# A hand-written instruction order for the first two batches: scores before maxima products, and norm rows before value transposes

## The reference

```
# layer 0: x is (256, 512) per batch; 8 heads of 32, over 512 positions, masked by cond
q      = x.T @ Wq.T                          # query, key and value are the same
logits = (scale * q q.T masked by key) * query mask
x      = x + (softmax(logits) @ q @ Wo.T).T
# layer 1: rows of x (256 rows of 512); 16 heads of 32
scale, shift = split(cond @ W_emb + b_emb)   # the modulation
xn      = rms_norm(x, g_norm) * (1 + scale) + shift
q, k, v = split(xn @ W_qkv);  q, k = rms_norm per head
x       = x + o + o @ W_out                  # o = softmax(q k.T / sqrt(32)) @ v
```

## Time and profile before

| | |
|---|---|
| median of 3 runs | 1290.88 us (1289.24 to 1292.41) |
| profiled execution | 1290.69 us |
| its span, first to last instruction | 1288.5 us |
| mean granted TensorE clock | 0.981 |
| busy in the span: TensorE, VectorE, ScalarE, GpSimd | 1231.0, 1032.1, 768.5, 771.6 us |
| instructions | 20732 |

### The profile page before, as it was taken

One profiled execution on the slowest core, in us unless ns is written; L12 is line 12 of the kernel. 1 busy time (PEld: TensorE's weight loads), 2 busy tenths in 40 slices (PEclk: granted clock), 3 DMA queues, 4 the chain that ended last, 5 costly groups with the idle time before them and its releaser, 6 DMA issues.

```text
span 1288.5 us, 20732 instructions
## 1 busy us (share of the span) xinstructions
PE 1231.0 (96%) x6769; PEld 577.5 (45%) x6769; DVE 1032.1 (80%) x920; ACT 768.5 (60%) x1394; POOL 771.6 (60%) x387
## 2 busy tenths in 40 slices
PE   3889899999999999999999999999999999999998
PEld 1364444545444454544445454444544444454434
DVE  6666878788887878888787888878888897887664
ACT  1616566766656576665657656565766656566524
POOL 1517566484756748575574857557485755837542
PEclk7969999999999999999999999999999999999999
DMA  5712635435373543536354353635345363533432
GB/s 143 266 34 75 155 92 123 110 88 125 82 171 92 120 111 83 133 82 168 95 117 110 87 132 82 163 97 116 95 102 138 82 161 93 119 91 74 98 73 59
DMA packets 77975, 143.00 MB, mean 111 GB/s; under 512 B 21552, under 2 KB 23088, under 8 KB 77872
## 3 DMA queue, kind: packets, MB, share of 16 engines
q1 hardware_dynamic: 69552, 130.36, 40.5%
q10 hardware_dynamic: 8320, 11.32, 3.3%
HBM read 32.02 MB, written 8.39 MB: 31 GB/s over the span
## 4 chain that ended last, share of the span: by engine, by line
PE 80%; POOL 6%; DVE 4%; issue 3%; ACT 3%; SPq 2%; DMA 1%; ACTq 1%; DVEq 0%; POOLq 0%
PE PX L599 25%; PE PS L501 9%; PE PO L531 8%; PE PX L633 8%; PE PS L518 5%; PE PO L553 5%; POOL RQK L2272 4%; PE PM L464 4%; PE PX L570 2%; PE PM L570 2%; PE PO L556 2%; PE PM L473 2%; SPq L2453 2%; PE PM L542 1%; PE PM L581 1%
## 5 line engine op out<-in xcount | busy, mean ns | idle before, releaser
L1213 ACT ACTIVATE E<-PS,KBIAS 128x512 f32<-128x512 f32 x512 | 340.8, 686 | 195.8 <-PE PS L501 152.6
L599 PE MATMUL PX<-WQKV,XNT 128*128 128x512 f32 x752 | 377.2, 604 | 0.7 <-DVE XNT L1895 0.4
L1822 DVE TENSOR_REDUCE NM<-PM 128x4 f32<-128x2048 f32 x128 | 292.1, 2282 | 72.3 <-PE PM L464 72.3
L2260 POOL TENSOR_TENSOR E<-E 128x1024 f32<-128x1024 f32 x112 | 263.3, 2370 | 88.1 <-PE PO L531 77.8
L501 PE MATMUL PS<-B,A 97*128 97x512 f32 x512 | 287.5, 597 | 4.6 <-ACT E L1213 3.8
L2290 POOL TENSOR_TENSOR KQLO<-E 128x1024 f32<-128x1024 f32 x64 | 151.6, 2368 | 224.4 <-ACT E L1220 222.7
L2272 POOL TENSOR_TENSOR RQK<-RQK,HALF 128x16 f32<-128x16 f32 x64 | 212.8, 3331 | 94.7 <-DVE RQK L1910 94.3
L1220 ACT ACTIVATE E<-PS 128x512 f32<-128x512 f32 x256 | 146.9, 597 | 110.6 <-PE PS L518 110.4
L599 PEld LDWEIGHTS PX<-WQKV,XNT 128*128 128x128 f32 x752 | 134.0, 191 | 99.7 <-issue 89.7
L1829 DVE TENSOR_REDUCE NM<-PM 128x8 f32<-128x2048 f32 x64 | 146.3, 2286 | 37.1 <-PE PM L473 37.1
L501 PEld LDWEIGHTS PS<-B,A 97*128 97x128 f32 x512 | 92.2, 189 | 156.5 <-issue 105.2
(11 more groups left out here) (87 smaller groups left out, 1352.4 us busy)
## 6 DMA issues: line engine op xcount, KB each, us to landing
A<-KQHI SPq DMA_DIRECT2D x126, 128.0 KB, 2.4
B<-KQHI SPq DMA_DIRECT2D x126, 128.0 KB, 2.4
A<-QHI SPq DMA_DIRECT2D x248, 64.0 KB, 2.0
B<-QHI SPq DMA_DIRECT2D x248, 64.0 KB, 2.0
XB<-x SPq DMA_DIRECT2D x16, 512.0 KB, 4.1
X<-x ACTq DMA_DIRECT2D x16, 512.0 KB, 5.0
out<-X1R SPq DMA_DIRECT2D x32, 256.0 KB, 2.9
A<-KQLO SPq DMA_DIRECT2D x63, 128.0 KB, 2.4
```

Source lines behind the costliest of these rows:

```text
L599: last = mm(bank, XNT[:, c, t * P:(t + 1) * P], WQKV[:, c, part * DM:(part + 1) * DM], start=(c == 0), stop=(c == 3))
L1213: fn(E[:, probs(seg, i, g), h, :], PS[n % 2][:, :], ACT.Exp, bias=KBIAS[:, g, b:b + 1], scale=SCALE).then_inc(exp_done, 1)
L1822: v.tensor_reduce(NM0[:, q, :].rearrange("p (h k) -> p h k", k=KB0)[:, :, kb], PM[:, :, :], axis=AX.X, op=ALU.max, negate=True).then_inc(m ...
L2260: g_.tensor_tensor(running(seg, i)[:, heads_, :], running(seg, i)[:, heads_, :], E[:, probs(seg, i, g), heads_, :], ALU.add).then_inc(done, 1)
```

## The change

It edits the order of iterations 0 and 1 on three engines, and the list of the banks' uses to match.

At the start of a batch (batch 0 here), on TensorE: scores 0 and 1 of segment A go in front of the second maxima product of quad 1. The first half of the next batch's query projection, which stood between score 0 and score 1, goes behind the third maxima product.

At the end of batch 0: the fourth maxima product of the next batch's quad 0 goes in front of the two output projections, on VectorE in front of the two residuals. Modulation slices 5, 6 and 7 now follow the output projections in one piece. `norm_rows` goes in front of the first `values0` of batch 1, and on ScalarE `modulate` in front of the copy that belongs to it.

```
@@ MAXES, special order 0 @@
-            (("q0", 1), 1, QUAD), (("q0", 2), 1, QUAD), (("w0", 1), 0, 3), (("q0", 3), 1, QUAD), (("n0", 0), 1, 0),
-            (("t0", 0), 1, 0), (("t1", 0), 0, 1), (("t1", 1), 0, 2), (("t0", 1), 1, 3), (("q1", 0), 1, QUAD),
+            (("q0", 1), 1, QUAD), (("q0", 2), 1, QUAD), (("q0", 3), 1, QUAD), (("w0", 1), 0, 3), (("n0", 0), 1, 0),
+            (("t1", 0), 0, 1), (("t1", 1), 0, 2), (("t0", 0), 1, 0), (("t0", 1), 1, 3), (("q1", 0), 1, QUAD),
@@ TensorE, iterations_0_and_1 @@
                 maxima0(i, i, 1, 0)
+                score0("A", i, i, 0, 0, 0)
+                score0("A", i, i, 0, 0, 1)
                 maxima0(i, i, 1, 1)
-                score0("A", i, i, 0, 0, 0)
-                project0(i, i + 1, 0)
-                score0("A", i, i, 0, 0, 1)
                 values0(i, i, 0)
                 score0("A", i, i, 0, 0, 2)
                 score0("A", i, i, 0, 0, 3)
                 maxima0(i, i, 1, 2)
+                project0(i, i + 1, 0)
                 score0("A", i, i, 0, 1, 0)
...
                 modulation(4)
+                maxima0(i, i + 1, 0, 3)
                 out0(i, i, 0)
                 out0(i, i, 1)
-                modulation(5)
-                maxima0(i, i + 1, 0, 3)
-                modulation(6, 7)
+                modulation(5, 6, 7)
                 rows0(i, i + 1, 0)
+                norm_rows(i, i)
                 values0(i + 1, i + 1, 0)
-                norm_rows(i, i)
                 values0(i + 1, i + 1, 1)
@@ ScalarE @@
                 rows0(i, i + 1, 0)
+                modulate(i, i)
                 values0(i + 1, i + 1, 0)
-                modulate(i, i)
                 exp0("A", i + 1, i + 1, 0, 0)
```

## The result

The changed kernel takes 1296.0 us in the median of 19 runs (1290.9 to 1301.1), the kernel before 1291.55 in 19 runs on the same chip (1289.2 to 1295.1). The ratio is 1.0024, with a 95% interval of 1.0014 to 1.0035: **slower by 3.1 us** (1.8 to 4.5), where I had forecast +0.4 us, 1291.1 with a range up to 1294.2. As a ratio it is inside the 0.3% that I had called "within", but clear of no change. The median itself, 1296.0, lies beyond the range. The two medians are 4.45 us apart, more than the ratio says: the runs of the changed kernel fall into two lots, 6 from 1290.9 to 1293.2 and 13 from 1295.3 up, and the median falls into the upper one. So a single pair of profiles must be read with care. All figures are of fast runs; one run of the experiments, of E2 (1315.2 us at a granted clock of 0.932), was slow and is left out.

The account below looks back on a forecast made before the run. TensorE, busy 96% of the span, was taken to bound the kernel; only the first key projection's shift counted. Terms +1.1 + 1.4 + 0.3 - 2.4 = +0.4 us on 1290.7 gave 1291.1, range 1288.2 to 1294.2.

Parts of the forecast that it names:

- So both scores fit in front of 31.7 us: Start of batch 0: both scores fill TensorE's idle time; the second maxima product starts at 31.7 instead of 31.32.
- The size of the first place: Scores and projection, 28 to 42 us: exponential 4 comes 1.5 us later, of which +1.1 us is carried.
- The bound of +2.5: Scores and projection, 28 to 42 us: the worst cost, if the clock rises only once the projection is over.
- The 0.4 us that I let ScalarE's idle time before exponential 6 absorb: Start of batch 0: ScalarE's 0.39 us of idleness takes up part of the 1.5 us shift, leaving +1.1.
- The clock at the first place: Start of batch 0: the clock rises near 39.4 instead of 36.0, 4.5 us after unbroken work begins at 34.9.
- Rival 2: Start of batch 0: clock still low behind about 42 us, +4.7 us in all, 1295.4; chance 0.13.
- (a): End of batch 0: the fourth maxima product moved ahead delays the output projection from 81.02 to 82.45, +1.4 us.
- (b): End of batch 0: the shifted pair of output projections needs +0.3 us more from the clock, between -0.3 and +1.8.
- (c): Output projection's end to first key projection: 6.2 us instead of 8.66, so -2.4 us (-1.3 at the low clock).
- the upper bound: Range's top: +2.5 at the start of batch 0 and +1.0 low clock at its end, 1293.1, plus run spread.
- rivals 1 and 3 together: Clock rises at 36 anyway (0.17) and doesn't fall at 66 to 69 us (0.12): 1287.0; faster than that, 0.07.
- The passing on of the offset: Behind both edited stretches: the first key projection's shift passes on whole; behind 140 us nothing moves but the offset.

Follow-up runs that it names:

- E2: Kernel before with only the edits at the end of batch 0, not those at the start of a batch; +0.3 us (-1.2 to +1.7).
- E9: Changed kernel with second quad's stacks issued behind the first row of maxima's landing and modulation weights behind the second's; +0.8 us against the kernel before.
- E1: Kernel before with only the edit at the start of a batch (scores 0 and 1, and the projection); +3.1 us (+1.4 to +4.7).
- E13: Kernel before with only the start-of-batch edit, plus two unused matmuls (512 and 256 columns) behind the second maxima product; +1.3 us.
- E7: Kernel before with only the end-of-batch-0 edits, and GpSimd's mask of the next batch's second half put before its power; -1.2 us.
- E10: Kernel before with second quad's stacks issued behind the first row of maxima's landing and modulation weights behind the second's; -0.3 us.
- E14: Changed kernel with the transfers of E9 and the two unused matmuls of E13; +0.4 us against the kernel before.
- E3: Kernel before with only scores 0 and 1 moved ahead of the second maxima product, the projection staying right behind that product; +1.6 us.
- E11: Kernel before with the start-of-batch order of E3, the end-of-batch-0 edits of E7 and the transfers of E9; -0.4 us.

## Why the prediction was wrong, point by point

**The step that failed** is the sentence on the first place, "So both scores fit in front of 31.7 us", with its conclusion that the second maxima product "then starts at about 31.7 instead of 31.32". The landing was right in absolute time (30.8 forecast from the earlier trace rows; 29.6 to 30.5 in the other profiles with the old transfers). The absolute times of the forecast nearly came true: second maxima product 31.7 (measured 31.10), TensorE idle to 34.9 (34.3), exponential 4 at 40.8 (41.34). What failed is what they were compared with. The mistake was to read the landing beside this one execution's VectorE, whose reduction ended at 31.27, and to cost the wait at 0.4 us. The profiled execution of before had a slow start, with its row transpose at 27.27. In 10 of the 15 other profiles of this study it came between 24.4 and 25.2, while with the old transfers the landing stayed near 30. There the maxima product is held 1.9 to 2.5 us in the four profiles with both moves and the old transfers. In a quick start the old order has exponential 4 at 37.20 (E2) and the new one at 41.06 to 41.34: the change takes back what the quick start had won. I had added up what is queued behind score 0 but not asked how much earlier the chain around the transfer can be. Across the experiments, keeping the rows clear is worth about 2.3 us of the 3.1 (changed kernel against E9, give or take some 2).

**The size of the first place**: +1.1 forecast (1.5 at exponential 4), +3.1 in time measured, +3.9 to +4.5 at exponential 4 counted from the row transpose. The bound of +2.5 left it out, since it was made of the clock alone and held the landing fixed beside the reduction. An estimate: 10 quick starts of 16 at +3.9 to +4.1, and the others at the forecast's +1.5, give about 3 us on average. No profile has the new order with the old transfers in a slow start, so the second term is the forecast's. The 0.4 us that I let ScalarE's idle time before exponential 6 absorb was not there: it still idled 0.28, and from exponential 4 to the first modulation product all but 0.15 to 0.3 us was passed on. The text also has 2.3 us of the projection covered by the reduction; by its own rows it is 1.8 (32.64 to 34.46), which no sum uses.

**The clock at the first place**: forecast to rise near 39.4. In the changed kernel's profile it rose at about 41.0, 6.7 us after the unbroken work began at 34.3, where before it had been 4.7; in E1's at 39.9. The projection took 3.78 us and 3.37, for 3.4 at the low clock. The Trainium skill, page "TensorE: Matmul & The Clock Gate", Part 1, says that sustained activity releases the throttle; E13 agrees, and more directly than the trace of before did: with two added matmuls the rise comes at about 34 us, against about 40 in E1. Rival 2, the late clock, had the right direction and named 1295.4, close to the 1296.0 measured, but that is luck: it decides from a rise later than 42 us, and the profile has it at 41.0.

**Second place, (a)**: +1.4 forecast, +1.44 to +1.47 in every profile with this edit. **(b)**: +0.3 forecast; the pair took 5.4 to 6.0 us in the seven profiles with this edit. In the nine without it it took 5.05 to 6.66, and the mean is 5.7 in both lots. So no cost of the edit is shown here; the 5.05 of before was the shortest of all. **(c)**: -2.4 forecast against the 8.66 of before, -1.4 in E2 (7.28) and -2.37 in E7 (6.29). The missing 1.0 is the norm slowed beside the mask. Without the edit this stretch varies too, from 7.6 to 8.8 us, short where the pair ahead of it was long; so the whole place, the table's last column, is the safer measure: 24.0 to 24.1 without the edit (25.7 in E10), 24.4 to 24.9 with it, 23.6 with the mask early. I had taken VectorE's half from where it stood before, behind the reduction and clear of GpSimd; moved forward it met the mask. The text had the sentence "GpSimd's order is untouched", and stopped there.

**Two sums of the text** are off, and 1296.0 lies outside with either figure: the upper bound adds up to 1293.5, not 1293.1, and rivals 1 and 3 together to 1287.5, not 1287.0.

**What came on top**: in 3 of the 7 profiles with the new second place (none of the two with the early mask) the clock stayed low under the key projection for some 5 us, and the stretch from it to the first heads' transpose took 28.9 us; in the nine profiles without it the longest was 27.3, the shortest 26.5. That is in the list of what would make the prediction wrong, but with no price. It costs up to 2.4 us when it happens, and the timed runs of E2 show little of it on average.

**The passing on of the offset** can't be judged from one pair. In this pair it held: +5.2 at 121 us, +5.7 at the end of the span, and nothing changed from 400 to 800 us (395.35 us of TensorE against 395.43). But from the first heads' transpose to the end, where all the kernels have the same order, the profiles take between 1167.3 us (before, the shortest) and 1173.6 (E14, in which the clock reads 0.67 from 836 to 840 us). E1 is +2.4 at 121 us and +6.5 at the end. That spread is larger than the whole effect, so the end of a single span says little, and only the timed runs carry the size.

**What stays open**: the exact split of the 3.1 us. Clearing the row and filling the gap recover 3.0 and 2.65 us of exponential 4 and together 4.2 (16.53 against 12.33 in E14), so they aren't terms to be added: a product that isn't held also brings the unbroken work, and with it the clock, forward. E3's +1.6 in time isn't explained by its profile. What makes the two lots of the changed kernel's runs is open. Quick and slow starts alone hardly explain them: with the landing near 30 us in both, the start should change little in this order. The low clock under the key projection, 2.4 us, and the spread behind 121 us are candidates; the timed runs show neither.

## What to carry to other kernels

A wait in an in-order queue costs what stands behind it, so before moving a step forward ask when its slowest input lands in absolute time, and compare that with the earliest time at which the work behind it could run, over several executions and not the one in the profile. A step that looks late may be cover for another engine's work; moving it can cost its whole length, and on TensorE the clock too. And where an operation moves in time, look at what runs beside it at the new time, as with VectorE and GpSimd here, where both were slower side by side.

## What the runs showed of the hardware that I had not expected

The landing of the small row's transfer took 1.8 us with the queues clear and 4.0 to 5.2 in quick starts with the stacks in front (in the changed kernel the transfer engines' share is 1.0 and more from 18 to 28 us). In slow starts, issued later, it took 2.7 to 3.2 us: issued at 25.5 it landed at 29.9, issued at 28.0 at 30.8.

VectorE's scaling of 128x512 took 0.48 us alone and 1.49 beside a GpSimd multiplication of 1.27 us that started 0.06 us before it, and 0.49 again when that multiplication was moved. The 1.49 is the rest of GpSimd's instruction (1.2) and about 0.3 more; waiting for all of it and then running alone would make 1.7. In E7 and E11 the mask, started at 66 to 67 us beside VectorE's work, took 2.25 us instead of 1.27. The Trainium skill, page "SBUF — State Buffer", section "SBUF: two separate sides", describes the pair of ports that VectorE and GpSimd share as a lock held for a whole instruction, and not as shared bandwidth; this trace agrees with it in kind, with 0.2 us less than a full block, and the length of a GpSimd instruction in the profile is rough.
